# Hyperbolic attention with a fused MLP: sums in four double transfers, and four steps moved in a hand-written order

## The reference, cut to what matters

```python
q_norm_sq = jnp.sum(q * q, axis=-1, keepdims=True)
k_norm_sq = jnp.sum(k * k, axis=-1)[..., None, :]
qk = jnp.einsum('bhnd,bhmd->bhnm', q, k)
diff_sq = q_norm_sq + k_norm_sq - 2.0 * qk
denom = (1.0 - c * q_norm_sq) * (1.0 - c * k_norm_sq)
denom = jnp.maximum(denom, 1e-06)
cosh_arg = jnp.maximum(1.0 + 2.0 * c * diff_sq / denom, 1.0)
dist = jnp.arccosh(cosh_arg)
attn = jax.nn.softmax(-dist, axis=-1)
out = jnp.einsum('bhnm,bhmd->bhnd', attn, v)
...
x = x + _L1_attn_ref(_layernorm(x), wq, wk, wv, wo)      # 16 heads of 8
x = x + relu(_layernorm(x) @ w1 + b1) @ w2 + b2          # width 512
```

## Time and profile before

| | |
|---|---|
| median of 3 runs | 2448.92 us |
| the profiled execution's own time | 2456.33 us |
| its span, first to last instruction | 2454.2 us |
| granted TensorE clock over the span | 0.907 |
| busy TensorE / VectorE / ScalarE / GpSimd | 85 / 80 / 72 / 66% |
| the fused loop | from about 1341 us to 2405 us |

### The profile page before, as it was taken

One profiled execution on the slowest core, in us unless ns is written; L12 is line 12 of the kernel. 1 busy time (PEld: TensorE's weight loads), 2 busy tenths in 40 slices (PEclk: granted clock), 3 DMA queues, 4 the chain that ended last, 5 costly groups with the idle time before them and its releaser, 6 DMA issues. The chain is left out here.

```text
span 2454.2 us, 50808 instructions
## 1 busy us (share of the span) xinstructions
PE 2089.9 (85%) x15438; PEld 1566.8 (64%) x15438; DVE 1956.8 (80%) x5939; ACT 1767.4 (72%) x3085; POOL 1627.2 (66%) x1866
## 2 busy tenths in 40 slices
PE   4999999999999996999997677777777778777876
PEld 4677777777777775888885445555555555555554
DVE  4677776776777774778775899999999999999992
ACT  2666666666666762444432799999999999999996
POOL 2776676766666750000001899999999999999993
PEclk7999999999999996999997579888888988889888
DMA  5000000000000003353450466776666777666674
GB/s 142 1 2 2 2 1 2 2 1 2 1 2 1 2 2 70 86 119 76 96 114 10 93 127 130 139 138 128 124 119 127 141 141 134 119 129 124 129 142 80
DMA packets 81388, 184.24 MB, mean 75 GB/s; under 512 B 9479, under 2 KB 31530, under 8 KB 81195
## 3 DMA queue, kind: packets, MB, share of 16 engines
q0 software_dynamic: 36864, 134.23, 29.1%
q1 hardware_dynamic: 36010, 43.38, 7.9%
q10 hardware_dynamic: 8320, 4.19, 0.7%
HBM read 42.85 MB, written 4.72 MB: 19 GB/s over the span
## 5 line engine op out<-in xcount | busy, mean ns | idle before, releaser
L1557 POOL TENSOR_TENSOR spare<-spare,u 128x1024 f32<-128x1024 f32 x192 | 456.2, 2376 | 16.0
L542 ACT ACTIVATE prob<-s_ps,nmax 128x128 f32<-128x128 f32 (+1 forms) x1024 | 364.4, 432 | 132.2 <-DVE nmax L599 132.2
L599 DVE CUSTOM_DVE_ANT_0 s_ps<-s_ps,mask 128x128 f32<-128x128 f32 (+1 forms) x1024 | 340.7, 385 | 100.7 <-issue 76.4
L1633 DVE TENSOR_SCALAR u<-d_ps 128x1024 f32<-128x1024 f32 x256 | 312.1, 1219 | 48.7 <-PE i_ps L1374 48.1
L579 POOL TENSOR_TENSOR g_lo<-g_all,g_hi 128x512 fp32r<-128x512 f32 x256 | 329.1, 1286 | 21.4
L1637 DVE SCALAR_TENSOR_TENSOR u<-i_ps,u 128x1024 f32<-128x1024 f32 x256 | 313.5, 1225 | 13.2 <-DVE u L1633 0.5
L1374 PE MATMUL d_ps<-rowsT 28*128 28x256 f32 x1024 | 144.7, 357 | 149.5 <-DVE u L1637 145.9
L534 ACT COPY g_all<-g_ps 128x512 f32<-128x512 f32 x256 | 151.5, 592 | 162.6 <-PE g_ps L63 161.5
L1514 ACT ACTIVATE u<-u 128x1024 f32<-128x1024 f32 x256 | 257.0, 1056 | 1.7 <-DMA u<-spare 1.6
L1517 ACT ACTIVATE u<-u 128x1024 f32<-128x1024 f32 x256 | 255.7, 1051 | 0.0
L1374 PEld LDWEIGHTS d_ps<-rowsT 28*128 28x128 f32 x1024 | 92.4, 208 | 246.3 <-issue 241.7
(11 more groups left out here) (275 smaller groups left out, 5795.2 us busy)
## 6 DMA issues: line engine op xcount, KB each, us to landing
u<-spare POOLq DMA_DIRECT2D x256, 512.0 KB, 12.2
w_all<-w_rows SPq DMA_DIRECT2D x128, 256.0 KB, 5.9
x<-L_attn_x ACTq DMA_DIRECT2D x8, 512.0 KB, 13.9
y<-x SPq DMA_DIRECT2D x32, 128.0 KB, 10.0
wkqv<-L_attn_Wkqv SPq DMA_DIRECT2D x4, 528.0 KB, 8.9
gate_rows<-L_ffn_gate_proj SPq DMA_DIRECT2D x1, 512.0 KB, 14.4
up_rows<-L_ffn_up_proj SPq DMA_DIRECT2D x1, 512.0 KB, 11.1
down_cols<-L_ffn_down_proj SPq DMA_DIRECT2D x1, 512.0 KB, 13.0
```

The costliest lines, as they stand in the source:

```text
L542: last = nc.scalar.activation(prob[:, kind, at, :].rearrange("p c n -> p (c n)"), s_ps[kind][:, at.start * P:at.stop * P], ACT.Exp, bias=n ...
L599: last = nc.vector.tensor_tensor_reduce(out=scores, in0=scores, in1=keep.mask[:, N - width:N], scale=-1.0, scalar=3.4e38, op0=ALU.add, op1 ...
L1557: nc.gpsimd.tensor_tensor(extra, extra, pair, ALU.mult).then_inc(prod_done, 1)
L1633: nc.vector.tensor_scalar(u[:, slot(i, p), :], d_ps[:, :], 0.0, None, ALU.max).then_inc(dist_done, 1)
```

## The change

It has six parts, all in the fused loop.

1. Sums: four DMAs of two pairs each (128 x 2048) in place of eight of one. The first three go out behind the sixth product, the fourth (pairs 6 and 7) behind the first product of the next batch. The norm of the MLP's input stands behind the third.
2. Products: u+2 is one instruction of 1024 columns; the four-column addition and its tile `twos` are gone. There are still six products.
3. TensorE turns the next batch's rows 0 behind the seventh pair (p = 6) and no longer at p = 5, rows 1 behind the attention output, and rows 2 at p = 7, behind the next batch's first pair products.
4. VectorE's features stand behind the sixth ratio (p = 5), no longer the fifth.
5. VectorE adds the MLP's output behind the third ratio (p = 2), no longer the second.
6. ScalarE reads the second half of the hidden layer between the logarithms and the exponentials of pairs 4 and 5, no longer ahead of them.

```diff
-    SUMS_BEHIND = {5: (0, 1, 2, 3, 4, 5, 6, 7)}
+    SUMS_BEHIND = {5: (0, 2, 4)}
...
+    FEATURES_AT = 5
...
         def wait_sum(engine, b, p):
-            after(engine, sum_landed[p], 16 * (b + 1))
+            after(engine, sum_landed[p // 2], 16 * (b + 1))
...
         def pool_sum(pool, b, p, i):
-            pool.wait_ge(root_done, b * HP + p + 1)
-            nc.gpsimd.dma_start(u[:, slot(i, p), :], spare[:, p, :], accum_op=ALU.add).then_inc(sum_landed[p], 16)
+            pool.wait_ge(root_done, b * HP + p + 2)
+            at = slot(i, p)
+            nc.gpsimd.dma_start(u[:, at:at + 2, :], spare[:, p:p + 2, :], accum_op=ALU.add).then_inc(sum_landed[p // 2], 16)
...
-            nc.gpsimd.tensor_tensor(extra[:, 0:4], pair[:, 0:4], twos[:, :], ALU.add)
-            nc.gpsimd.tensor_scalar(extra[:, 4:2 * W2], pair[:, 4:2 * W2], 1.0, 2.0, ALU.mult, ALU.add).then_inc(raised, 1)
+            nc.gpsimd.tensor_scalar(extra, pair, 1.0, 2.0, ALU.mult, ALU.add).then_inc(raised, 1)
...
-                            for r in {5: (0,), 6: (1,), 7: (3,)}.get(p, ()):
+                            for r in {6: (0,), 7: (2, 3)}.get(p, ()):
                                 pe_turn_rows(pe, b + 1, r)
...
-                            for r in {6: (2,), 7: (4,)}.get(p, ()):
+                            for r in {6: (1,), 7: (4,)}.get(p, ()):
                                 pe_turn_rows(pe, b + 1, r)
...
-                def weights(b, i, p):
-                    for logarithm in (True, False):
-                        for n in range(2):
-                            act_weights(act, b, p + n, i, logarithm)
+                def weights(b, i, p, relu_of=None):
+                    for n in range(2):
+                        act_weights(act, b, p + n, i, True)
+                    if relu_of is not None:
+                        act_relu(act, relu_of, 1)
+                    for n in range(2):
+                        act_weights(act, b, p + n, i, False)
...
                         if four_before and p == 2:
-                            for half in range(2):
-                                act_relu(act, b - 4, half)
+                            act_relu(act, b - 4, 0)
...
                     for p in PRODUCTS:
                         pool_product(pool, b, p, i)
+                        if p == 0 and one_before:
+                            pool_sum(pool, b - 1, HP - 2, (i - 1) % TURN)
...
-                        if p == 1 and five_before:
+                        if p == 2 and five_before:
                             dve_y(dve, b - 5)
...
-                            if p == 4:
+                            if p == FEATURES_AT:
                                 after(dve, relu_done, 2 * (b - 3))
                                 dve_features(dve, b + 1)
```

More of the change, by code:

```diff
@@ L1272, in hyperbolic_attention_and_mlp @@
         attnT = m.sb("attnT3", [P, N])
-        twos = m.sb("twos", [P, 4])
         part_stats = m.sb("part_stats3", [P, TURN, TB, 6])
@@ L1311, in hyperbolic_attention_and_mlp @@
         prod_done, root_done, ln_done, w_done, pv_done = S_("prod_done"), S_("root_done"), S_("ln_done"), S_("w_done"), S_("pv_done3")
-        sum_landed = [S_(f"sum_landed{n}") for n in range(HP)]
+        sum_landed = [S_(f"sum_landed{n}") for n in range(HP // 2)]
         o_copied, o_turned, rec_done, attn_done = S_("o_copied3"), S_("o_turned3"), S_("rec_done3"), S_("attn_done3")
@@ L1833, in body @@
                         if one_before:
-                            weights(b - 1, (i - 1) % TURN, p)
+                            weights(b - 1, (i - 1) % TURN, p, b - 4 if four_before and p == 4 else None)
                         if one_after and p in (0, 2):
@@ L1879, in _ @@
                 nc.gpsimd.memset(v[:, :, :, :, DH:VW], 1.0).then_inc(zeroed, 2)
-                nc.gpsimd.memset(twos[:, :], 2.0).then_inc(v_cleared, 1)
                 nc.gpsimd.memset(eps[:, :], LN_EPS).then_inc(rows_set, 1)
                 nc.gpsimd.memset(xh4[:, :, :, :], 1.0).then_inc(rows_set, 1)
-                pool.wait_ge(v_cleared, 3)
                 pool.wait_ge(rows_set, 2)
@@ L1892, in body @@
                             pool_sum(pool, b, n, i)
-                            if n == NORM4_BEHIND and three_before:
-                                pool_norm4(pool, b - 3, i)
+                        if p == NORM4_BEHIND and three_before:
+                            pool_norm4(pool, b - 3, i)
                 written_out(body)
+                pool_sum(pool, END, HP - 2, END % TURN)
                 for b in (END - 2, END - 1, END):
                     pool_norm4(pool, b, b % TURN)
-                for p in range(HP):
+                for p in range(0, HP, 2):
                     wait_sum(pool, END, p)
```

## The result

The changed kernel takes 2476.91 us (median of 5 runs, 2468.59 to 2477.81) against 2448.92 for the kernel before: ratio 1.0101, 95% interval 1.0079 to 1.0123. It is slower by 28 us. Forecast were 2464 us, in a range of 2440 to 2486, with 0.6 for slower.

The account below looks back on a forecast made before the run. No engine was taken as saturated; three stood within 5% of the batch period, with VectorE and TensorE in a ring. Per batch +0.94 - 0.95 = -0.01, plus 0.5 for half clocks, over 31 batches +15 us on 2448.92: 2464 us, range 2440 to 2486.

Parts of the forecast that it names:

- Rows 2, +0.94 us a batch at full clock and +1.61 at half: Rows 2 turned behind the next batch's first products delay VectorE's copy and first distance, in each of 31 batches.
- The half-clock term, +0.5 us: TensorE at half clock around the late turn: about 1.1 us in about half the batches, bounds 0 and 1.1.
- Its place: Where TensorE's clock falls: behind some 1.8 us idle in one piece ahead of the next batch's first products.
- The savings of VectorE, -0.95: Moved features and MLP output shorten VectorE's waits for pair products and MLP output: -0.95 us a batch, bounds -1.05 and -0.3.
- longer ring: VectorE and TensorE wait on each other: products need the ratio before, distances need products; longer than ScalarE's 32.03 plus seams.
- ScalarE's hidden wait: ScalarE's wait for the hidden layer, 0.57 us a batch, goes, but is worth nothing while VectorE's ring is longer.
- Sums and products 0: GpSimd's merged transfers and wider scaling change nothing: 0 us a batch, bounds -0 and +1.0.
- The first (full clock keeps): Rival: the same exchange without the half-clock term, 2449 us, no change; chance 0.2.
- The second: Rival: rows 2's copy is covered, the loop is ScalarE's and gets 28 to 34 us faster, about 2418 us; chance 0.18.
- The third: Rival: sums or the wide scaling come late, ScalarE waits up to 1.0 us a batch, 2480 us and more; chance 0.1.

Follow-up runs that it names:

- experiment 1: Changed kernel with only rows 2 turned ahead of the next batch's first pair products again: 2416.91 us, ratio 0.989 to the kernel before.
- experiment 2: Kernel before with only the turning of rows 0 to 3 placed as in the changed kernel: 2480.38 us, ratio 1.014.
- experiment 8: Changed kernel with four filler products on TensorE, two ahead of the turning of the attention output and two behind: 2461.92 us, ratio 1.0056.
- experiment 10: Experiment 1's kernel with the hidden layer's second half read ahead of the logarithms again: 2431.46 us, ratio 0.9923 to the kernel before.
- experiment 5: Kernel before with only the sums and products changed (four transfers of two pairs, scaling 1024 columns wide): 2447.65 us, ratio 1.0002.
- 3: Changed kernel with VectorE copying rows 2 behind the next batch's first distance: 2466.67 us, ratio 1.0094 to the kernel before.
- 7: Changed kernel with seven filler products on TensorE around the sixth pair: 2477.24 us, ratio 1.012 to the kernel before.

## Why the prediction was right, and where its sizes were off

The sign and the mechanism are shown: experiment 1 takes the turn of rows 2 away and the loss with it, experiment 2 makes it alone and gets the loss alone. The forecast's 15 us against 28 measured is a matter of sizes, and some of their errors cancel.

- *Rows 2, +0.94 us a batch at full clock and +1.61 at half.* For the first distance of a batch both are right. From the eighth ratio's start to that distance's it takes 2.33 us before, 3.95 in the changed kernel at half clock (2047.23 to 2051.18), +1.62, and 3.19 at full clock (1597.76 to 1600.95 in experiment 8's trace), +0.86. For the whole batch it is less certain. The two batches of experiment 2 without any half clock take 33.1, about 0.6 more than the kernel before in its short batches (32.5). Experiment 8's full-clock batch takes 33.11 against 32.04 in experiment 1, +1.1, but carries four fillers. There ScalarE, which sets the pace in experiment 1, waits 1.1 us a batch in the five early batches: 3.8 us in all for the turned inputs and 1.8 for a transpose of rows.
- *The half-clock term, +0.5 us, is what was mis-sized.* The step put 1.1 us into about half of the batches. In experiment 8 such a batch costs 1.0 (34.10 against 33.11), so the price in one was about right. But every batch of the 20 is such. With 1.0 instead of 0.5 the sum is -0.01 + 1.0 = +0.99, 31 us, against 28 measured. The trace before could have said more of the share. In 20 of its 27 batches the clock is at half around the first pair products or just behind them, and 12 batches have a stretch of about 7 us at half. Those 12 took 33.6 to 35.8 us, most of them near 34.0, and the other 15 took 32.35 to 32.68. A neighbouring pair of them:
```profile
1834.35:1866.86 32.51, 24.38 (x220) 16.58 (x218) 31.04 (x63) 32.15 (x43) 31.80 (x32) 0.95 0.71 133
1866.86:1900.86 34.00, 27.17 (x220) 18.83 (x218) 31.32 (x62) 32.10 (x43) 31.72 (x32) 0.85 0.67 127
```
  So the kernel before had batches as long as the changed kernel's 34.1 already. The change made all of them so.
- *Its place was right for the turn alone, wrong for the change.* The step expected the fall behind an idle piece of 1.8 us ahead of the next batch's first products. With the turn alone it is there, behind 1.79 us (experiment 2). In the changed kernel it comes a pair earlier, behind 1.02 and 1.76 us around the features. The prediction counted the features' move only as a saving, and didn't ask what TensorE would do meanwhile. That move doesn't bring the fall by itself: experiment 1 has it, at a mean clock of 0.94.
- *The savings of VectorE, -0.95, were too large.* In the changed kernel the waits for pair products fell by 0.42, not 0.72. Measured by themselves, with rows 2 back and ScalarE's move undone, VectorE's moves gain 18 us (experiment 10), 0.57 a batch. With ScalarE's move (experiment 1) it is 30 us, 0.96 a batch, inside my bound of -1.05 but holding the hidden layer's part, which the prediction priced at nothing under a longer ring. (The traces give more, 33.29 to 32.04, but that of the kernel before is of an execution 7.4 us above the median.)
- *The terms don't add.* The turn alone costs 34 us, the other moves alone gain 30, and together they cost 28 and not 4. Next to the late rows 2 the other moves take 6 us off and no longer 30. The prediction priced each term in the old loop and added them up, which can't give that. Its savings were too large and its half-clock term too small, so that it still came out on the right side is in part luck.
- *ScalarE's hidden wait worth nothing here.* Right under the change's own ring; in experiment 1, where the ring is short, it is worth some 12 us.
- *Sums and products 0.* Right, to 0.1% (experiment 5). The full-width scaling takes 1089 ns, the narrower form took 1142. The Trainium skill (DMA: Bandwidth & Descriptors, Anatomy of one DMA) gives each such DMA a fixed cost of some 2 us; halving their number moved no time here, so a cost like that lies under the stream of the others.
- *Rivals.* The first (full clock keeps) was close to the truth for 5 batches of experiment 8's trace and for an early batch of the changed kernel: the one at 1534.75 took 32.83 us with a wait of 0.68. The second's price, a gain of 28 to 34 us, holds for experiment 1 with its 30. Its condition, a stall under some 0.5 us, isn't met at 0.77 or 1.52. The third did not occur: ScalarE waits for no transfer.

Open is why a batch takes 34.1 us in five kernels whose waits differ (the changed one, experiments 2, 3 and 7, the late part of 8). Three batches take 102.4 us in each but experiment 2, where they take 102.5. From 1669 us on the clock of the changed kernel falls and rises at the same places of every batch. It looks as if the loop and the clock's falls had settled on each other, so that a shorter wait is given back elsewhere; this is a guess, and no run isolates it. What is shown is that the late turn of rows 2 brings the loss. How that loss divides between the order and the half clock rests on one trace (experiment 8) and is open within some tenths of a us a batch.

## What to carry to other kernels

Where two engines feed each other in a ring, ask for each moved instruction whether it was filling time in which its engine waited anyway; a transpose taken out of such a gap and put behind the next product delayed the next distance here by more than its own length (0.86 us for 0.66), and TensorE's clock can fall around it as well. Price each edit by itself and then together: here one table entry hid a gain of 30 us in the rest. The version to keep is that of experiment 1, 2416.91 us, 1.1% under the kernel before. And the work taken off an engine with no wait behind it (GpSimd's 4.5 us a batch) was worth nothing here.

## What the runs showed of the hardware

- A transfer of 1 MB from GpSimd is issued in 0.88 us at the mean, and lands in 10.2 us at the median, where 512 KB landed in 12.2 in a fuller queue; the queue's share of the engines is 27.0% with half as many packets.
- TensorE's granted clock fell to 0.50 behind waits of only 1.02 and 1.76 us, with 0.76 us of work in 3.41 (in experiment 2 behind one of 1.79, with 0.28 in 1.71), and in the changed kernel stayed there for 10.2 us although TensorE was then busy in 9.69 of 10.24.
- One program ran its loop at two speeds in one execution (experiment 8), 33.1 to 33.5 and then 34.1 us a batch, with a switch at 1728 us and no difference in work.
